# A conditional residual kernel: its prologue in another order, the identity added to half the taps, quad 0 loaded in two transfers, the products' rows issued from two queues

## What is computed

```
x = x + conv1d(x, w0, 9 taps, 4 groups) + (cond @ cw.T)[:, :, None] + bias[None, :, None]
for n in (1, 2, 3):                       # three conditional 1x1 mixes
    h = gelu(gelu(cond @ W0 + b0) @ W1 + b1)
    att = softmax(h @ W2 + b2)            # (128, 8)
    x = x + einsum('boi,bih->boh', einsum('bk,koi->boi', att, weight_n), x) + (att @ bias_n)[:, :, None]
```

## Time and profile before

| | |
|---|---|
| median of 3 runs | 321.65 us (321.52 to 324.29) |
| profiled execution, its own time | 323.18 us |
| its span | 321.3 us |
| PE busy | 309.9 us, 96% |
| VectorE, ScalarE, GpSimd busy | 262.4, 228.2, 129.4 us |
| chain that ended last | PE 91%, DMA 3%, SP's queue 2%, ACT 1%, DVE 1% |
| granted clock of TensorE, mean | 0.993 |

### The profile page before, as it was taken

The page is one execution under the profiler, slowest core; times in us unless marked ns, Lnnn a source line. Parts: engine busy times, 40 slices in busy tenths (PEclk is TensorE's granted clock), DMA queues, the critical chain, the costliest instruction groups (busy, mean ns, idle before and its releaser), DMA issues.

```text
span 321.3 us, 6082 instructions
## 1 busy us (share of the span) xinstructions
PE 309.9 (96%) x1474; PEld 251.8 (78%) x1474; DVE 262.4 (82%) x290; ACT 228.2 (71%) x346; POOL 129.4 (40%) x271
## 2 busy tenths in 40 slices
PE   8787999999999999999999999999999999999993
PEld 8556878888888888888888888888888888888872
DVE  5664788889887889888889888898888888987883
ACT  5544677777777788776777777887777777778663
POOL 5510397454444333444433444434444333344400
PEclk9998899999999999999999999999999999999999
DMA  7787366999999999899999999999999999996687
GB/s 230 218 234 281 134 222 212 370 365 364 348 340 342 372 337 373 337 365 360 363 380 340 354 341 359 340 373 336 361 370 353 370 344 368 344 363 280 266 329 274
DMA packets 30946, 104.53 MB, mean 325 GB/s; under 512 B 3428, under 2 KB 4708, under 8 KB 23113
## 3 DMA queue, kind: packets, MB, share of 16 engines
q1 hardware_dynamic: 30938, 104.43, 88.0%
HBM read 36.26 MB, written 33.55 MB: 217 GB/s over the span
## 4 chain that ended last, share of the span: by engine, by line
PE 91%; DMA 3%; SPq 2%; ACT 1%; DVE 1%; issue 0%; DVEq 0%
PE bank L409 54%; PE bank L451 9%; PE bank L453 9%; PE bank L452 9%; PE bank L417 4%; DMA x_sb<-in_x 3%; PE bank L537 2%; SPq L283 2%; PE bank L459 1%; ACT x_hi L628 1%; PE bank L508 1%; PE bank L465 0%; DVE att L837 0%; PE bank L475 0%; PE bank L485 0%
## 5 line engine op out<-in xcount | busy, mean ns | idle before, releaser
L635 ACT ACTIVATE conv_sb<-bank 128x512 f32<-128x512 f32 x128 | 76.2, 596 | 62.9 <-PE bank L409 59.0
L355 POOL COPY a_diag<-table 64x64 f32 (+1 forms) x128 | 49.7, 388 | 132.2 <-PE bank L417 112.6
L762 DVE TENSOR_TENSOR x_lo<-x_sb,x_hi 128x2064 fp32r<-128x2064 f32 x31 | 71.5, 2308 | 24.5 <-ACT x_hi L628 23.3
L365 POOL COPY a_dup<-table 64x128 f32 (+1 forms) x128 | 70.9, 554 | 34.4 <-ACT table L680 16.9
L409 PE MATMUL bank<-x_hi,toep_hi 128*128 128x512 f32 x256 | 84.3, 411 | 0.1
L409 PE MATMUL bank<-x_lo,toep_hi 128*128 128x512 f32 x256 | 80.7, 397 | 0.0
L409 PE MATMUL bank<-x_hi,toep_lo 128*128 128x512 f32 x256 | 80.5, 395 | 0.0
L779 DVE TENSOR_TENSOR ybuf<-ybuf 128x1024 fp32r<-128x1024 f32 x62 | 77.1, 1244 | 1.1
L628 ACT ACTIVATE x_hi<-x_sb 128x2064 fp32r<-128x2064 f32 x32 | 61.7, 1928 | 11.3 <-DMA x_sb<-in_x 11.0
L655 ACT ACTIVATE out_sb<-bank,beta 128x512 f32<-128x512 f32 x93 | 63.4, 684 | 5.0 <-DMA out<-out_sb 1.8
L409 PEld LDWEIGHTS bank<-x_hi,toep_lo 128*128 128x128 f32 x256 | 48.3, 189 | 12.1
(11 more groups left out here) (95 smaller groups left out, 167.0 us busy)
## 6 DMA issues: line engine op xcount, KB each, us to landing
x_sb<-in_x SPq DMA_DIRECT2D x32, 1032.0 KB, 7.8
ybuf<-conv_sb SPq DMA_DIRECT2D x128, 256.0 KB, 5.0
out<-out_sb SPq DMA_DIRECT2D x29, 1024.0 KB, 7.9
out<-out_sb SPq DMA_DIRECT2D x8, 256.0 KB, 2.5
out_sb<-conv_sb SPq DMA_DIRECT2D x8, 128.0 KB
out<-x_sb SPq DMA_DIRECT2D x4, 256.0 KB, 3.4
x_sb<-in_toep SPq DMA_DIRECT2D x1, 640.0 KB, 6.1
early<-in_mixrow SPq DMA_DIRECT2D x1, 390.0 KB
```

The source lines that it names most:

```text
L355: nc.gpsimd.tensor_copy(a3_diag[rows, par, :, C * h + NH * e:C * h + NH * e + NH], table[0][C * e:C * e + C, here, h, :]).then_inc(comp_in, 1)
L365: nc.gpsimd.tensor_copy(a21_dup[rows, par, :, :, NH * e:NH * e + NH], table[1][C * e:C * e + C, here, h, :].unsqueeze(2).to_broadcast([C, ...
L635: nc.scalar.activation(conv_sb[:, par, g, :], conv_ps[g % banks][:, :], ACT.Copy).then_inc(conv_out, 1)
L762: nc.vector.tensor_tensor(x_lo[:, par].rearrange("p g s j -> p (g s j)"), x_sb[:, par].rearrange("p g s j -> p (g s j)"), x_hi[:, par].rea ...
```

## The change

- GpSimd: the identity is added only to the taps that it touches (for each of the two halves d, half of the four columns h), as two instructions over 256 elements each, in place of one over 1024. `toep_set` counts to 2.
- SP: quad 0 comes in two transfers of 516 KB (`x0_first`, then `x_in[0]`), and stands before, not behind, the four transfers of `mrow[0]`, which go to ScalarE's list, at its very start.
- The eight rows of products: even l from SP, odd l from ScalarE, there behind `product_copy` and ahead of `toep_hi`, with a wait for `pprod_dve` and `rows21_zero`.
- ScalarE: `x_hi` of quad 0 in two halves; `table_bank` and `conv_copy` of quad 0 interleaved; `vcol_copy(0)` ahead of `x_high(1, 0, 1)`.
- VectorE: `x_lo` of quad 0 in pieces of one, one and two groups; `x_low(1, 1)` later, behind `table_bank(11)`; `mix_low(0, 0)` ahead of the second `y_low`.
- PE: the first two convolutions wait only for the first halves; `bias_products(0)` between them and the other two; `tables(8)` ahead of `bias_turn(0)`.

The diff, cut to its core (of SP, GpSimd, PE and ScalarE):

```diff
@@ sync @@
-            sp.wait_ge(rows3_zero, 1)
-            for i in range(RT):
-                n = C * C // RT
-                sp.dma_start(mrow[0][32 * i:32 * i + K + 1], own_h[0:K + 1, n * i:n * i + n]).then_inc(rows3_in, 16)
-            load(0, 0)
+            n = G // 2 * S * JX
+            sp.dma_start(x_sb[:, 0, 0:G // 2].rearrange("p g s j -> p (g s j)"), x_h[0:128, 0:n]).then_inc(x0_first, 16)
+            sp.dma_start(x_sb[:, 0, G // 2:].rearrange("p g s j -> p (g s j)"), x_h[0:128, n:]).then_inc(x_in[0], 16)
...
-            for l in range(K):
-                sp.dma_start(mrow[1][l:l + RS * (K - 1) + 1:RS].rearrange("m (a n) -> m a n", a=CB),
-                             prod[:, l].rearrange("p c k -> p (c k)")).then_inc(rows21_in, 16)
+            for l in range(0, K, 2):
+                pair_row(sp, l)
@@ gpsimd @@
-            nc.gpsimd.tensor_tensor(taps, taps, eyes.to_broadcast([128, 2, G, 128]), ALU.add).then_inc(toep_set, 1)
+            for d in range(2):
+                h = slice(QP // 2 * d, QP // 2 * d + QP // 2)
+                nc.gpsimd.tensor_tensor(taps[:, d, :, :, h], taps[:, d, :, :, h],
+                                        eyes[:, d, :, :, h].to_broadcast([128, G, 2 * CG, QP // 2]), ALU.add).then_inc(toep_set, 1)
@@ scalar @@
+            act.wait_ge(rows3_zero, 1)
+            for i in range(RT):
+                n = C * C // RT
+                nc.scalar.dma_start(mrow[0][32 * i:32 * i + K + 1], own_h[0:K + 1, n * i:n * i + n]).then_inc(rows3_in, 16)
...
-            act.wait_ge(toep_set, 1)
+            act.wait_ge(rows21_zero, 1)
+            act.wait_ge(pprod_act, 3)
+            act.wait_ge(pprod_dve, 1)
+            for l in range(1, K, 2):
+                pair_row(nc.scalar, l)
+            act.wait_ge(toep_set, 2)
```

More of the change, by code:

```diff
@@ L189, in cond_resid_kernel @@
         x_in = [sem("x_in0"), sem("x_in1")]
+        x0_first, xhi_first = sem("x0_first"), sem("xhi_first")
         stored = [sem("stored0"), sem("stored1")]
@@ L239, in cond_resid_kernel, with pair_row @@
         block = ctx.enter_context(nc.Block())
+        def pair_row(eng, l):
+            eng.dma_start(mrow[1][l:l + RS * (K - 1) + 1:RS].rearrange("m (a n) -> m a n", a=CB),
+                          prod[:, l].rearrange("p c k -> p (c k)")).then_inc(rows21_in, 16)
         @block.sync
@@ L375, in _ @@
             taps = toep.rearrange("p (d g m) -> p d g m", d=2, g=G)
-            eyes = eye_tap.rearrange("p (d o m) -> p d o m", d=2, o=1)
-            nc.gpsimd.tensor_tensor(taps, taps, eyes.to_broadcast([128, 2, G, 128]), ALU.add).then_inc(toep_set, 1)
+            taps, eyes = (t.rearrange("p d g (m h) -> p d g m h", h=QP) for t in
+                          (taps, eye_tap.rearrange("p (d o m) -> p d o m", d=2, o=1)))
+            for d in range(2):
+                h = slice(QP // 2 * d, QP // 2 * d + QP // 2)
+                nc.gpsimd.tensor_tensor(taps[:, d, :, :, h], taps[:, d, :, :, h],
+                                        eyes[:, d, :, :, h].to_broadcast([128, G, 2 * CG, QP // 2]), ALU.add).then_inc(toep_set, 1)
             pool.wait_ge(toep_hi_set, 1)
@@ L402, in conv @@
                 if g == 0:
-                    pe.wait_ge(xhi_set, q + 1)
+                    pe.wait_ge(*((xhi_first, 1) if isinstance(q, int) and q == 0 else (xhi_set, q + 1)))
                     pe.wait_ge(*((xlo_first, 1) if isinstance(q, int) and q == 0 else (xlo_set, q + 1)))
@@ L550, in _ @@
             stream(3, 1)
-            bias_products(0)
             pe.wait_ge(toep_hi_set, 1)
@@ L556, in _ @@
             taken(BANKS.index(1))
+            pe.wait_ge(xlo_first, 2)
+            conv(0, 0, 1, banks=2)
+            bias_products(0)
+            pe.wait_ge(xhi_set, 1)
             pe.wait_ge(xlo_set, 1)
-            for g in range(1, G):
-                conv(0, 0, g, banks=2)
+            conv(0, 0, 2, banks=2)
+            conv(0, 0, 3, banks=2)
+            tables(8)
             bias_turn(0)
-            for t in (8, 9, 10):
-                tables(t)
+            tables(9)
+            tables(10)
             bias_products(1)
@@ L684, in _ @@
             product_copy(3, 1)
-            act.wait_ge(toep_set, 1)
+            act.wait_ge(rows21_zero, 1)
[4 more added lines that the diff above has]
+            act.wait_ge(toep_set, 2)
             nc.scalar.activation(toep_hi[:].rearrange("p d g m -> p (d g m)"), toep,
                                  ACT.Copy).then_inc(toep_hi_set, 1)
[L688 to L691, removed]
+            for there, g, done in ((x0_first, slice(0, G // 2), xhi_first), (x_in[0], slice(G // 2, G), xhi_set)):
+                act.wait_ge(there, 16)
+                nc.scalar.activation(x_hi[:, 0, g], x_sb[:, 0, g], ACT.Copy).then_inc(done, 1)
+            table_bank(0)
             conv_copy(0, 0, 0, 0, banks=2)
+            table_bank(2)
             conv_copy(0, 0, 0, 1, banks=2)
+            table_bank(4)
+            table_bank(6)
             conv_copy(0, 0, 0, 2, banks=2)
-            x_high(1, 0, 1)
-            vcol_copy(0)
             conv_copy(0, 0, 0, 3, banks=2)
             table_bank(8)
+            vcol_copy(0)
+            x_high(1, 0, 1)
             table_bank(10)
@@ L859, in _, with x_low_part @@
             table_bank(3)
+            def x_low_part(g):
+                return nc.vector.tensor_tensor(x_lo[:, 0, g], x_sb[:, 0, g], x_hi[:, 0, g].bitcast(F32), ALU.subtract)
+            dve.wait_ge(xhi_first, 1)
+            x_low_part(slice(0, 1)).then_inc(xlo_first, 1)
+            x_low_part(slice(1, 2)).then_inc(xlo_first, 1)
             table_bank(5)
             dve.wait_ge(xhi_set, 1)
-            for g, done in ((slice(0, 1), xlo_first), (slice(1, G), xlo_set)):
-                nc.vector.tensor_tensor(x_lo[:, 0, g], x_sb[:, 0, g], x_hi[:, 0, g].bitcast(F32),
-                                        ALU.subtract).then_inc(done, 1)
+            x_low_part(slice(2, G)).then_inc(xlo_set, 1)
             table_bank(7)
             bias_sum(0)
-            x_low(1, 1)
             table_bank(9)
@@ L871, in _ @@
             table_bank(11)
+            x_low(1, 1)
             table_bank(13)
@@ L876, in _ @@
             y_low(0, 0, 0)
+            mix_low(0, 0)
             y_low(0, 0, 1)
-            mix_low(0, 0)
             dve.wait_ge(vcol_set, NL)
```

## The result

| | before | after |
|---|---|---|
| median of 20 runs each, us | 321.93 (320.48 to 324.29) | 324.19 (322.05 to 325.69) |
| after / before | | 1.0061, 95% interval 1.0040 to 1.0082 |
| profiled execution: its time / its span, us | 323.18 / 321.3 | 324.4 / 322.6 |
| first convolution on PE, us | 16.96 | 20.95 |
| first `mix` of quad 0 on PE, us | 45.22 | 46.59 |

A forecast was written before the change was run, and what follows sets the result against it. PE is full in the steady loop, which the change leaves alone, so only the prologue counts: first convolution 19.15 + 24.4 to the mix + 1.6 for the clock = 45.15 against 45.22, hence 321.5 us, range 318.6 to 324.6.

The forecast's parts named there:

- Head: ScalarE's start: four issues ahead of the table load put the first Gelu at 4.7 us, +0.4 us on the chain.
- Identity: GpSimd's addition to the taps: halved, it no longer blocks VectorE's att, which ends 0.9 us earlier.
- Product rows: Row issues split over SP and ScalarE: four each take 2.6 us, both through at 14.8 us; no landing gain counted.
- the rival of hindering queues: Row issues on SP and ScalarE take turns, ending at 17.4 us: 324.1 us, or 325.8 with the head; 15%.
- The rule that I quoted: Issues on both queues: the Trainium skill's shared, locked descriptor generator would make row issues about 1.2 us each.
- The first rival, cheap issues: ScalarE's issues cost 0.1 us or less each, PE begins at 16.9 us: 318.5 to 320.1 us; 22%.
- What stands behind the four issues: ScalarE's toep_hi, then toep_lo and the low part, come later: first convolution at 19.15 us where it was 16.96.
- Load of quad 1: SP's load still issued at 18.35 us, landing at about 27; PE's 1.43 us wait for vcol goes.
- From the first convolution to the mix: PE's prologue: three waits and the slow clock go, one bias product is added, 24.4 us in place of 28.26.
- Clock: PE's first convolutions: the clock falls after 4.3 us of idle and costs 1.6 us, bounds 0 and 3.0.
- the rival that the clock stays low through them: PE's clock stays at its lower level through all four first convolutions: 322.9 us; 7%.
- Sum: Start of quad 0's first mix on PE: 45.15 us against 45.22, a change of -0.1 us, so 321.5 us.

The follow-up runs named there:

- a4: Changed kernel with the four mrow[0] transfers issued by SP again, ahead of quad 0: 324.09 us, ratio 1.0073 to the kernel before.
- a2: Changed kernel with ScalarE's four product-row issues moved behind toep_hi and x_hi: 324.06 us, ratio 1.0032 to the kernel before.
- a3: Changed kernel with 28 instead of 3 blank matmuls ahead of the first convolution: 322.31 us, ratio 1.0005 to the kernel before.
- a5: Changed kernel with ScalarE's row issues behind toep_hi and x_hi, and SP's loads held until all rows landed: 317.6 us, ratio 0.9835 to before.
- a1: Changed kernel with all eight product rows issued by SP, without ScalarE's waits for them: 317.32 us, ratio 0.9856 to before; again 317.47, 0.9864.
- b1: Kernel before with only the identity added in two parts over half the columns: 322.30 us, ratio 1.0014 to the kernel before.
- b2: Kernel before with only the vcol copy and quad 0's fourth copy ahead of quad 1's rounding on ScalarE: 323.0 us, ratio 0.9979.
- d1: Changed kernel with all product rows on SP and the identity added to all 1024 columns at once: 319.04 us, ratio 0.9868 to before.
- b3: Kernel before with the vcol copy ahead of quad 1's rounding and VectorE's x_low of quad 1 later: 319.89 us, ratio 0.9935.
- c1: Changed kernel with all product rows and the four mrow[0] transfers on SP: 319.14 us, ratio 0.9892 to the kernel before.

## Why the prediction was right and wrong

The path was right: ScalarE's issues, `toep_hi`, `toep_lo`, the low part, then PE, behind an idle stretch that costs the clock. The steps that failed are terms of its sum. The products' last copy ended at 12.90 where I had 12.1, the four issues on ScalarE took 3.71 us where I had 2.6, and the clock cost 2.3 where I had 1.6. That makes the start of the mix 2.5 us later than forecast, and it was only 1.4 later because another term, the way from the first convolution to the mix, was 1.1 too long. This second error hides part of the first by luck.

*Head: mis-sized, 0 where I took +0.4.* The issues took 1.69 us and the first Gelu came at 4.74, as worked out. But PE caught up: its six products behind it began at 5.25 and took 1.08 us, and those of the logits (L494) began at 7.49, where they had begun at 7.62. a4 shows no gain from an earlier head.

*Identity: gain 0.1 where I took 0.9.* Three terms failed. The taps landed at 9.67 in place of 8.64; each of the two additions took 0.82 and not 0.6 us; and `att` was free (0.18), but by luck: it ran before the additions began, not behind them as I had it, and left the block to its followers. GpSimd and VectorE, after:

```profile
9.67 1.64 POOL L385 TENSOR_TENSOR x_sb<-x_sb 128x256 f32<-128x256 f32 x2 [5.01 <-DMA x_sb<-in_toep]
```

```profile
9.48 0.18 DVE L862 TENSOR_TENSOR att<-expo,recip 128x24 f32<-128x24 f32 x1
9.77 0.82 DVE L869 TENSOR_TENSOR mix_f<-att 128x64 f32<-128x64 f32 x1
10.51 0.82 DVE L870 COPY mix_f<-att 128x16 f32<-128x16 f32 x1
11.25 0.17 DVE L871 COPY mix_f<-att 128x32 f32<-128x32 f32 x1
```

I had looked at the one instruction that was blocked before and not at those behind it, which read from SBUF just as it does. The products' last copy ended at 12.90, not at 12.1. Which of them is blocked changes from trace to trace: in a2, the same up to here, the taps landed at 9.83, `att` and its followers were through by 10.01, none was blocked, and the copy ended at 11.49. Why the taps landed later isn't settled: with the own transfers on SP they came at 8.4 to 9.4, on ScalarE's queue at 8.8 to 9.8, over all kernels here, and these ranges overlap.

*Product rows: the mechanism right, the price too low.* ScalarE's issues, in a row from 13.02, took 3.71 us in place of 2.6. Issues at L244 in the kernel after (ns min/median/max, first and last start us):

```profile
L244 SPq DMA_DIRECT2D out_sb<-conv_sb x4: 617/658/762, 13.0 to 15.1; - x4
L244 ACTq DMA_DIRECT2D out_sb<-conv_sb x4: 712/805/1295, 13.0 to 15.4; - x4
```

In a2, where they overlapped SP's least, ScalarE's median was 630 ns, about SP's own price. Beside SP the medians were 805, 814 and 890 ns in the changed kernel, a3 and a4, and 682 in a5; the last of the four took 1.1 to 1.7 us in these. So the rival of hindering queues was partly right: 1.3 to 1.4 times a2's median in the first three, not the double. Its 324.1 us meets the measured 324.19 by luck: it had the issues end at 17.4 and they ended at 16.73, and the rest came from the late copy and the clock. The rule that I quoted, of a lock on the generator inside the issue's span, fits the direction and not the size. The long last issue isn't explained. The first rival, cheap issues, is out; by the terms of my own sum PE would have reached the rows there at 16.9 + 5.6 + 0.9 = 23.4 and not at 23.8.

*What stands behind the four issues: the step that decided, right.* `toep_hi` began where the issues ended (16.77), `toep_lo` ended at 20.25, and the first piece of the low part, ready at 18.81, ended at 20.82: it took 2.01 us where 0.70 is its price, and waited for GpSimd as I let it. In a1, where it started at 14.76, behind `toep_lo`'s end at 14.66, both pieces together took 1.29. GpSimd, after:

```profile
17.90 2.35 POOL L388 TENSOR_TENSOR toep_lo<-x_sb,toep_hi 128x1024 fp32r<-128x1024 f32 x1 [6.60 <-ACT toep_hi L708]
```

All three are 1.9 us later than forecast, by the 0.8 and the 1.1 us of the two steps above. The first convolution: 20.95 and not 19.15.

*Load of quad 1: late, without effect.* It was issued at 20.28 and not at 18.35, since it waits for `toep_lo`: the 1.9 us of the step before, passed on. PE did not wait for it, nor for vcol.

*From the first convolution to the mix: the waits right, the rest 1.1 too long.* None of the three waits came back. Measured are 46.59 - 20.95 = 25.6 us, without the clock's 2.3 so 23.3 (as in a3), where I had 24.4. I had taken the idle stretches off but not the slower restart behind each: bias products 1.13 us after a wait and 0.86 without one, the tables 2.94 and 2.68 (after: 33.68 to 36.36 in the chain). That is 0.5 of it. Another 0.5 are the tails: an instruction in a row is overlapped by the next by about 0.15 us (46.09 + 0.64 against the mix at 46.59), and ahead of each of the three waits it was not. The last 0.1 I did not follow up.

*Clock: the fall right, its price 2.3 in place of 1.6.* I had taken the price paid after two stretches of 1.4 to 1.5 us for one after 4.3 us, which was 5.6 in the end. The clock stood at its lower level for 5.1 us of PE's work (20.95 to 26.1), and before for some 3.4 (30.4 to 33.8, by the granted clock); half of either is near its price. My upper bound was wrong too: two convolutions take 2.84 us at full clock, so all four at half rate would cost some 5.7 us and not 3.0, and the rival that the clock stays low through them would have been at 325.6, not 322.9. With the convolution that starts 0.36 later, a3 won 2.0 us at the mix and 1.9 by the medians.

*Sum.* Against the forecast: first convolution +1.8, the clock +0.7, the rest of the way to the mix -1.1. That is 46.59 where 45.15 was forecast and 45.22 stood before; the span moved by 1.3. The median moved by 2.0, 0.6 more than the trace of one execution explains. The execution traced before was itself 1.3 us above its median (323.18 against 321.93), the one after 0.2 (324.40 against 324.19), so this pair of traces shows less than the medians do; the interval (1.3 to 2.6) holds both, and what else there may be I leave open.

## What to carry to other kernels

A DMA issue is work of the engine that makes it: 0.3 to 0.5 us each for the small ones here, 0.6 to 0.9 for most of the product rows and up to 1.7, in order with all else on that engine. Before giving issues to a second engine, look at what stands behind them there, and put them behind the operation that others wait for. Then look at what the first queue will issue earlier because of it: it shares the DMA engines with the rows that were to be sped up. And when a wait is removed, follow its engine's list to the next instruction that needs the same input or port, as with `att` and its followers, or vcol and `x_low`: twice here an edit alone won nothing (b1, b2), and by the traces it paid beside others (a1 against d1, b3).

## What the runs showed of the hardware

Transfers on two queues aren't served in the order of their issue. With the 2 MB of quads 1 and 2 issued on SP's queue from 15.08, rows issued on ScalarE's by 16.0 landed at 30.2; with the loads held back, at 22.3. Behind each other on one queue (a1) rows issued until 18.1 were in at 22.7, although the same 2 MB followed at once. The 30.2 is of one trace, but the medians of a2 and a5 point the same way. On one queue the landing isn't fixed either: with all rows on SP, PE got them 4.6 us (a1) to 8.1 us (c1) behind the end of the last issue, and nothing here says why. The Trainium skill says in "DMA: Bandwidth & Descriptors", section "Issuing engines are not separate DMA queues", that transfers of several engines interleave on the same 16 engines; these runs agree, and show what it can cost.

A VectorE copy of 32 elements a partition, from SBUF to SBUF, took 2.33 us in b3 while GpSimd added, and 0.17 in the changed kernel, where GpSimd was through:

```profile
9.45 2.33 DVE L846 COPY mix_f<-att 128x32 f32<-128x32 f32 x1
```

The Trainium skill, in "SBUF — State Buffer", section "Who interferes with whom", names copies in a two-port mode, beside operations with two inputs in SBUF, as those that GpSimd can block for a whole instruction. The row agrees: blocked are not only two-operand instructions, as I had assumed, and which one it hits is a matter of a few tenths of a microsecond.
